# Two input loads of the first pass, issued in parts by rows of partitions

## The reference

```
x0 = x
x  = groupnorm(x, 32 groups)                 # mean and variance of each group of 16 channels
xl1 = relu(batchnorm(depthwise conv of x with w1 over the height))   # (2, 512, 1, 256)
xl2 = relu(batchnorm(depthwise conv of x with w2 over the width))    # (2, 512, 256, 1)
num = softmax(linear(linear(sum(xl1 * xl2))))                        # one number for a batch and channel
out = x0 + x * num
```

## Time and profile before

| | |
|---|---|
| median of 3 runs | 1701.75 us (1701.73 to 1702.97) |
| the profiled execution: its own time | 1705.46 us |
| its span in the trace | 1703.7 us |
| busy: DVE, ACT, POOL, PE | 60%, 39%, 30%, 28% of the span |
| DMA: moved, mean rate | 721.71 MB, 424 GB/s |
| chain that ended last | DMA 43%, unknown queue 26%, DVE 6% |

### The profile page before, as it was taken

One profiled execution on the slowest core, in us unless ns is written; L12 is line 12 of the kernel. 1 busy time (PEld: TensorE's weight loads), 2 busy tenths in 40 slices (PEclk: granted clock), 3 DMA queues, 4 the chain that ended last, 5 costly groups with the idle time before them and its releaser, 6 DMA issues.

```text
span 1703.7 us, 14479 instructions
## 1 busy us (share of the span) xinstructions
PE 482.9 (28%) x3464; PEld 174.9 (10%) x3464; DVE 1015.8 (60%) x2714; ACT 656.8 (39%) x510; POOL 508.4 (30%) x474
## 2 busy tenths in 40 slices
PE   3588766650223313233223334510000000000000
PEld 1123212220001100011001111300000000000000
DVE  5899999988675757767575886872222222222220
ACT  4688887863643545544355555600000000000000
POOL 7688787830233445434154000000000000000000
PEclk8799977885666656566666656665555555555555
DMA  9999999989999999999999999999999999999999
GB/s 390 421 428 426 426 427 427 426 354 413 431 432 430 430 430 431 430 430 430 430 431 430 429 430 430 404 375 432 432 431 432 431 432 431 431 431 431 431 431 396
DMA packets 51983, 721.71 MB, mean 424 GB/s; under 512 B 6225, under 2 KB 6737, under 8 KB 8018
## 3 DMA queue, kind: packets, MB, share of 16 engines
q1 hardware_dynamic: 33922, 458.84, 63.6%
q10 hardware_dynamic: 18000, 262.15, 36.1%
HBM read 452.53 MB, written 268.44 MB: 423 GB/s over the span
## 4 chain that ended last, share of the span: by engine, by line
DMA 43%; another core or an unknown queue 26%; DVE 6%; PE 3%; issue 2%; ACT 2%; SPq 1%; POOL 0%; DVEq 0%; ACTq 0%; POOLq 0%
DMA xs<-in_x 31%; DMA out<-xs 11%; DVE xs L1194 3%; PE ps_part L608 2%; DVE xs L1059 1%; SPq L392 1%; ACT xs L905 1%; ACT sq_junk L825 1%; DVE y2s L1062 1%; DVE filters L1033 1%; PE ps_part L731 0%; POOL rstd_b L490 0%; PE ps_l L724 0%; DVE mul_junk L1033 0%
## 5 line engine op out<-in xcount | busy, mean ns | idle before, releaser
L825 ACT ACTIVATE sq_junk<-xs 128x4096 fp8e5<-128x4096 f32 x128 | 463.1, 3618 | 213.9 <-DMA xs<-in_x 209.8
L1194 DVE TENSOR_SCALAR xs<-xs,scale,shift 128x4096 f32<-128x4096 f32 x91 | 226.2, 2507 | 358.8 <-DMA xs<-in_x 358.2
L608 PE MATMUL ps_part<-xs,filters 128*32 128x512 f32 x1792 | 279.3, 779 | 521.2 <-DMA xs<-in_x 511.8
L1033 DVE SCALAR_TENSOR_TENSOR xs<-xs,ps_w 128x256 f32 (+1 forms) x832 | 294.8, 417 | 29.0 <-DMA xs<-in_x 19.6
L552 POOL TENSOR_TENSOR xs<-xs,w_late 128x2048 f32<-128x2048 f32 x40 | 179.7, 4524 | 102.9 <-ACT w_late L839 102.9
L905 ACT ACTIVATE xs<-xs,shift,scale 128x4096 f32<-128x4096 f32 x32 | 121.5, 3797 | 154.7 <-DVE xs L1194 123.6
L608 PEld LDWEIGHTS ps_part<-xs,filters 128*32 128x32 f32 x1792 | 75.4, 138 | 706.9 <-issue 706.9
L1059 DVE TENSOR_TENSOR xs<-xs,ps_w 128x4096 f32<-128x4096 f32 x26 | 114.7, 4412 | 55.3 <-PE ps_part L608 52.6
L1053 DVE TENSOR_REDUCE y2s<-xs 128x8 f32<-128x2048 f32 x40 | 91.4, 2286 | 77.4 <-POOL xs L552 77.4
L453 POOL TENSOR_TENSOR xs<-xs 128x768 f32<-128x768 f32 x64 | 116.7, 1826 | 58.5 <-DMA xs<-in_x 55.5
L490 POOL TENSOR_TENSOR rstd_b<-var,minus_half 128x2 f32<-128x2 f32 (+1 forms) x22 | 14.5, 658 | 386.1 <-DVE var L1091 386.1
(11 more groups left out here) (138 smaller groups left out, 488.7 us busy)
## 6 DMA issues: line engine op xcount, KB each, us to landing
xs<-in_x SPq DMA_DIRECT2D x208, 2048.0 KB, 24.1
out<-xs ACTq DMA_DIRECT2D x120, 2048.0 KB, 27.0
filters<-in_x SPq DMA_DIRECT2D x5, 2048.0 KB, 15.8
out<-filters ACTq DMA_DIRECT2D x5, 2048.0 KB, 88.6
out<-xs SPq DMA_DIRECT2D x3, 2048.0 KB, 19.9
xs<-in_lw SPq DMA_DIRECT2D x2, 2048.0 KB, 16.6
filters<-in_w_rows SPq DMA_DIRECT2D x1, 512.0 KB, 4.0
filters<-in_w SPq DMA_DIRECT2D x1, 512.0 KB, 9.2
```

The lines of the kernel that those rows point to most:

```text
L608: last = nc.tensor.matmul(ps_part[g % 2][32 * a:32 * a + 32, :], taps[:, g % 2, hf * JH + j, :], xs[:, s[0]:s[1] + 1:s[1] - s[0], j * W:(j ...
L825: nc.scalar.activation(sq_junk[:], xs[:, s, :], ACT.Square, accum_out=sq_sum[:, u % 2, u // 2, b:b + 1], saturate=False).then_inc(squared, 1)
L1033: return nc.vector.scalar_tensor_tensor(out=out, in0=x_row, scalar=1.0, in1=ps_w2[g % 2][:, 0:W], op0=ALU.mult, op1=ALU.mult, accum_out=total)
L1194: return nc.vector.tensor_scalar(buffer(s), buffer(s), scale[:, b, g:g + 1], shift[:, b, g:g + 1], ALU.mult, ALU.add)
```

## The change

Two loads of batch 1 are issued in parts. Unit 12 goes as two transfers, of partitions 0 to 119 and of 120 to 127. Unit 20 goes as 16 transfers of 8 partitions each. The bytes, their place in SBUF and the order of the loads stay. Every part adds 16 to the slot's semaphore, and `landed` counts the parts, so that a reader waits for all of them. No engine but SP has another instruction; waits have other constants.

```diff
+def rows_of(key):
+    if key == ("x", 12, 1):
+        return [slice(0, 120), slice(120, P)]
+    if key == ("x", 20, 1):
+        return [slice(p, p + 8) for p in range(0, P, 8)]
+    return [slice(0, P)]
+
+
 def landed(slot, key):
-    return 16 * (LOADS[slot].index(key) + 1)
+    return 16 * sum(len(rows_of(k)) for k in LOADS[slot][:LOADS[slot].index(key) + 1])
...
-                sp.dma_start(xs[:, s, :], x_v[u // 2, :, b, part_of(u)]).then_inc(x_loaded[s], 16)
+                for rows in rows_of(("x", u, b)):
+                    sp.dma_start(xs[rows, s, :], x_v[u // 2, rows, b, part_of(u)]).then_inc(x_loaded[s], 16)
```

## The result

The changed kernel takes 1735.05 us (median of four, 1731.70 to 1738.41) where the kernel before, run on the same chip, takes 1702.05: a ratio of 1.019 [1.0178, 1.0203], or 33 us. Forecast was 1707.4, in a range from 1704.0 to 1710.0. The direction is right, and the size is short by a factor of six. The profiled execution took 1734.7 us, with a span of 1733.0, which is 29.3 us over the span before.

A forecast was written before the change was run, and what follows sets the result against it. The prediction took the work of one late DMA engine to bound the kernel. Nine more rows on it (5.5 us) and extra ends (0.1 us) add 5.6 us to 1701.75, giving 1707.4 us, in a range from 1704.0 to 1710.0.

The forecast's parts named there:

- The bound: From 30 us to the end: one DMA engine with practically no idle time sets the pace, not the sum over 16.
- The late engine is one of the eight: Units 12 and 20: the engine everybody waits for is among the eight that gain 9 rows; 85 in 100.
- The price of a row: Loads of units 12 and 20: 0.616 us a row on the late engine, so nine rows cost 5.5 us.
- What hides it: First pass to the end: nothing hides the late engine's added work, so the whole runs 5.6 us longer, bounds 4.6 and 6.5.
- SP: Issuing unit 20's parts: sixteen issues take 5.3 to 12 us against 11.1 us of room, so cost 0.
- DVE's cover of 0.92 us: First pass: DVE runs 0.92 us behind the last landing and can hide only a smaller shift; used once, 4.6 us remain.
- Relieved: Units 12 and 20: late engine is in the other half and loses 8 or 16 rows; 1696.4 us, chance 11 in 100.
- absorbed: Late engine has hidden slack, or slot waits pace the second pass; at most 0.9 us shows, 1702; chance 8 in 100.
- Dearer parts: Split loads: each one-row transfer holds its engine 0.3 us longer, or a full queue holds SP; 1712.5 us, chance 7 in 100.

The follow-up runs named there:

- extra8: Kernel before plus eight extra transfers behind unit 20, its lower 64 partitions again into a free slot: 1706.90 us against 1702.40, 1.0027.
- pair8: Kernel before with unit 20 loading only partitions 0 to 7 and 32 to 39, in 8 two-partition parts: 1697.29 us against 1702.40, 0.9967.
- lower8: Kernel before with unit 20 loading only its lower 64 partitions, in 8 parts of 8 partitions four apart: 1703.17 us against 1701.87, 1.0003.
- lower7: Kernel before with unit 20 loading only partitions 0 to 27 and 32 to 59, in 8 parts of 7: 1702.52 us against 1702.40, 0.9998.
- low4: Kernel before with unit 20 loading only partitions 0 to 15 and 32 to 47, in 8 parts of 4: 1702.36 us against 1702.69, 0.9996.
- only120: Kernel before with only unit 12 split, as 120 and 8 partitions, unit 20 whole: 1712.39 us against 1703.03, 1.0058.
- only16: Kernel before with only unit 20 split, as 16 parts of 8 neighbouring partitions, unit 12 whole: 1723.57 us, 1.0120.
- up2: Kernel before with unit 20 loading only partitions 64 to 71 and 96 to 103, by two engines: 1703.67 us, 1.0004.
- up4: Kernel before with unit 20 loading only partitions 64 to 79 and 96 to 111, in 8 parts of 4: 1712.98 us against 1702.69, 1.0061.
- upper8: Kernel before with unit 20 loading only its upper 64 partitions, in 8 parts of 8 partitions four apart: 1714.97 us, 1.0066.
- spread16: Kernel before with unit 20 as 16 parts of 8 partitions, each taking every fourth of 32: 1719.66 us against 1703.03, 1.0093.
- src_spread: Kernel before with unit 20 as 16 parts, each writing 8 neighbouring partitions but reading rows four apart: 1723.97 us, 1.0129.
- dst_spread: Kernel before with unit 20 as 16 parts, each reading 8 neighbouring rows but writing partitions four apart: 1717.30 us against 1701.87, 1.0085.

## Why the prediction was wrong

Step by step:

*The bound* was right. One engine without idle time sets the end: extra8 moves the end by what 8 rows take, pair8 gives 8 rows back, and relief of the other eight, nine or twelve gives nothing (lower8, lower7, low4).

*The late engine is one of the eight* (85 in 100) was right. The packet counts of the earlier trace rows were a fair reading, though no run shows that the order at 38 us is what made it late at 343.

*The price of a row*, "0.616 us a row. Nine rows are 5.5 us", is the step that failed. The number is right for rows written where engines usually write them: extra8. The prediction held it for every row of the changed transfers and for every row of other loads beside them. The runs put in its place 1.23 us a row on all 16 engines for some 14 us at unit 12, and 1.17 on average for 24 us at unit 20: 33 us instead of 5.6. Behind it is the sentence "What changes is which DMA engine moves which row": so it also changes which partitions an engine writes and which rows it reads, and no row of the trace before could price that, since every transfer there has one and the same pattern. The prediction should have bounded it as an operation that isn't shown, by the only other patterns, the affine transfers of the earlier trace rows, and left the top of the range open.

Sized again, in rates: unit 12 in only120 runs at 209 to 223 GB/s from 142 to 154 us and at 324 and 346 in the four us on either side. Against 427 this is worth 7.6 us, and 0.6 for the one row more: 8.2, of a landing that moved by 10.2 and a time that moved by 9.4. Unit 20 in only16 runs below 427 from 219 to 247, worth 10.6 us (windows of 4 us, 262, 287, 205, 205, 234, 283 and 383 GB/s), and 4.9 for eight rows: 15.5 of 19 to 20.5 us. The rest, some 4 to 5 us, lies by this estimate where the engines run dry behind it: from 205 to 340 us they stood idle for some 5 us on average. In only16 the share is 0.73, 0.51 and 0.67 from 247 to 259; the middle one:

```profile
251.00:255.00 4.00, 3.86 (x20) 1.15 (x24) 3.51 (x19) 3.71 (x2) 3.93 (x4) 0.50 0.51 217
```

That the late engine idled there too was not shown by itself.

*What hides it*: nothing, as forecast. DVE's cover of 0.92 us took nothing visible off.

*SP*: issues cost nothing, as forecast (17 in 5.86 us; lower8). That "an issue 1 us late lies in a queue with some 15 us ahead of it" was true of the time before. With the landing some 15 us late SP waited up to 22 us at a time, and a stretch with a share of 0.51 followed.

*The rivals.* "Relieved" and "absorbed" did not come. "Dearer parts" had the direction, but neither place nor size: it had the small transfers hold their own engine 0.3 us longer, and lower8 shows that they don't. What is dear is not small: a tile as 120 and 8 partitions costs 9 us, as twice 64 it costs 12.

By the Trainium skill's swizzle section a tile in parts of 8 neighbours has eight engines write into two ports at a time, where a full tile has one engine for each of 16. This was the rule that spoke against the change, and the prediction did not weigh it. By it alone a part of eight neighbours would be slow for the eight engines. It says nothing of the slowing of the other eight, and pair8, with two engines in one port at full rate, does not bear out that two in a port must be slow; the page's section "Back-pressure in remote DMA" speaks, for another path, of a full destination port that holds up engines that share the way to it. up2 is in keeping with that, but no run here separates it from other causes.

## What stays open

Why two engines with rows in the other half slow all sixteen, while two that share partitions within a half don't. Whether it is writing the upper half that does it, or reading the source's upper rows: low4 and up4 differ in both, and a run that reads one half and writes the other would tell. And whether a tile in parts could be free: all patterns tried that cover the tile cost 12 us or more at unit 20, and those that cost nothing (lower8, lower7, low4) leave rows out. A version that beats the kernel before did not come out: pair8 does, but only by leaving 112 rows of a tile out.

## What to carry to other kernels

Where DMA engines are the bound, be wary of cutting a 128-partition transfer by partitions, evenly or not: all five cuts of a whole tile cost 9 us or more here. A cut along the free dimension would let each engine keep its own partitions, but it wasn't run. Read the rate beside the share: a share of 1.00 at half the rate means that each row takes twice as long, and not that there is more to move. And before pricing a transfer of a new shape by the rows of an old one, ask which rows each engine will read and write, not only how many.

## What the runs showed that was not expected

- Engines of the lower eight with rows of partitions 64 to 127 bring all 16 from 414 to 434 GB/s down to 209 to 217, even when they are only two (up2, up4, upper8). The same engines with the same parts in 0 to 63 cost nothing (low4, lower8).
- Whether a part's partitions are neighbours or four apart matters on the write side (only16 262 GB/s at 219 to 223 us, spread16 385), and not on the read side (src_spread as only16, dst_spread as spread16).
- Small transfers with one 16 KB row for each engine are free when queued: eight of them in lower8, 1.0003 [0.9993, 1.0013].
- Twelve engines can lose 8 rows each of a tile with no gain (low4, 0.9996 [0.9986, 1.0006]), while one engine's 8 rows are worth 5 us at the end: 1697.29 against 1702.40 (pair8).
